# Linear attention in a fused attention and expert layer: head sums laid out place first, with the key sums as a ninth place, and the projection written to the other parity's bank

## The reference

```python
def _linear_attention(x, Wq, bq, Wk, bk, Wv, bv, Wo, bo):
    B, S, D = x.shape; H = 16; hd = D // H            # hd = 8
    v = (x @ Wv + bv).reshape(B, S, H, hd)
    q = elu((x @ Wq + bq).reshape(B, S, H, hd)) + 1.0
    k = elu((x @ Wk + bk).reshape(B, S, H, hd)) + 1.0
    def step(carry, qkv):                             # over the 256 tokens
        s, z = carry; q_i, k_i, v_i = qkv
        s = s + einsum('bhd,bhm->bhdm', k_i, v_i)
        z = z + k_i
        qs = einsum('bhd,bhdm->bhm', q_i, s)
        qz = einsum('bhd,bhd->bh', q_i, z)[..., None]
        return (s, z), qs / (qz + 1e-06)
    ...
    return values @ Wo + bo

x = x + layernorm(linear_attention(layernorm(x)))
x = x + layernorm(ffn(layernorm(x)))                  # shared expert + top-1 of 16
```

## Time and profile before

| | us |
|---|---|
| median of three runs | 351.48 |
| the profiled execution | 353.47 |
| its span, first to last instruction | 351.6 |
| stage 1, to the last quotient of attention | about 154 |
| busy over the span: PE, DVE, ACT, POOL | 266.0, 284.8, 188.8, 193.1 |

### The profile page before, as it was taken

The page is one execution under the profiler, slowest core; times in us unless marked ns, Lnnn a source line. Parts: engine busy times, 40 slices in busy tenths (PEclk is TensorE's granted clock), DMA queues, the critical chain, the costliest instruction groups (busy, mean ns, idle before and its releaser), DMA issues.

```text
span 351.6 us, 6328 instructions
## 1 busy us (share of the span) xinstructions
PE 266.0 (76%) x1493; PEld 189.3 (54%) x1493; DVE 284.8 (81%) x1147; ACT 188.8 (54%) x572; POOL 193.1 (55%) x221
## 2 busy tenths in 40 slices
PE   0449899999999995838887988730999999999100
PEld 0215565565656552524555755520999988988000
DVE  3599999999999999996998786560279999999940
ACT  1723566565656652447666563301799888885000
POOL 5064677777677773300055556371006888888870
PEclk9998999999999999877999899965699999999855
DMA  4999960000000000000011111126960101110100
GB/s 112 334 427 348 352 203 0 2 3 0 2 0 2 2 0 0 1 3 0 0 63 61 62 62 61 62 76 196 358 207 15 34 30 36 39 36 32 31 2 0
DMA packets 20275, 28.60 MB, mean 81 GB/s; under 512 B 2285, under 2 KB 15476, under 8 KB 19856
## 3 DMA queue, kind: packets, MB, share of 16 engines
q1 hardware_dynamic: 16624, 21.57, 18.2%
q0 software_dynamic: 3040, 6.37, 5.3%
q10 hardware_dynamic: 576, 0.26, 0.3%
HBM read 15.57 MB, written 13.60 MB: 83 GB/s over the span
## 4 chain that ended last, share of the span: by engine, by line
PE 39%; DVE 21%; POOL 17%; issue 12%; DMA 5%; ACT 1%; another core or an unknown queue 1%; SPq 1%; POOLq 0%; ACTq 0%; DVEq 0%
PE banks L1019 13%; POOL out L484 10%; POOL rows L478 5%; PE banks L1042 5%; DMA rows<-in_x 4%; PE banks L1106 3%; PE banks L1140 2%; PE banks L1048 2%; DVE hT L824 2%; POOL sorted_rows L468 2%; PE banks L1007 2%; PE banks L1040 1%; PE banks L1065 1%; PE banks L1063 1%; DVE stats L859 1%
## 5 line engine op out<-in xcount | busy, mean ns | idle before, releaser
L443 POOL TENSOR_TENSOR kv<-qk,vv 128x1024 f32<-128x1024 f32 x32 | 62.5, 1952 | 2.5
L1019 PE MATMUL banks<-kv,upto 128*128 128x512 f32 x128 | 61.3, 602 | 0.8 <-POOL kv L443 0.8
L1140 PE MATMUL banks<-xsT,w_now 128*128 128x128 f32 x376 | 53.8, 288 | 0.4 <-issue 0.4
L484 POOL DMA_INDIRECT out<-rows,token_i x47 | 46.9, 998 | 9.6 <-issue 8.0
L437 POOL TENSOR_TENSOR qk<-ex,rl 128x256 f32<-128x256 f32 x32 | 23.3, 729 | 50.4 <-ACT ex L542 50.4
L1140 PEld LDWEIGHTS banks<-xsT,w_now 128*128 128x128 f32 x376 | 48.1, 200 | 1.2 <-issue 0.5
L468 POOL DMA_INDIRECT sorted_rows<-rows,slot_i x32 | 31.6, 986 | 30.2 <-DVE slot_i L814 22.2
L728 DVE TENSOR_TENSOR prod<-banks,qk 128x1024 f32<-128x1024 f32 x32 | 38.9, 1217 | 2.7 <-PE banks L1019 0.8
L750 DVE TENSOR_REDUCE num<-prod 128x128 f32<-128x1024 f32 x32 | 38.7, 1208 | 0.3 <-DVE den L745 0.3
L958 DVE TENSOR_TENSOR hT_e<-silu_e,banks 128x256 f32<-128x256 f32 x47 | 19.3, 412 | 19.6 <-ACT silu_e L619 14.9
L478 POOL TENSOR_TENSOR rows<-rows,yn 128x128 f32<-128x128 f32 x40 | 19.2, 481 | 28.4 <-DVE yn L950 26.6
(11 more groups left out here) (152 smaller groups left out, 660.6 us busy)
## 6 DMA issues: line engine op xcount, KB each, us to landing
sorted_rows<-rows SPq DMA_DIRECT2D x3, 1950.0 KB, 12.0
rows<-sorted_rows SPq DMA_DIRECT2D x11, 520.0 KB, 6.2
w_exp<-in_gate_up SPq DMA_DIRECT2D x4, 1024.0 KB, 9.2
w_exp_down<-in_down SPq DMA_DIRECT2D x8, 256.0 KB, 8.8
out<-rows,token_i POOLq DMA_INDIRECT x47
rows<-in_x SPq DMA_DIRECT2D x1, 512.0 KB, 8.9
sorted_rows<-rows,slot_i POOLq DMA_INDIRECT x32
rows<-sorted_rows SPq DMA_DIRECT2D x1, 390.0 KB, 5.4
```

The costliest lines, as they stand in the source:

```text
L443: nc.gpsimd.tensor_tensor(kv[:, u, :].rearrange("p (h m d) -> p h m d", h=NH, m=HD), k, v, ALU.mult).then_inc(s_kv, 1)
L484: nc.gpsimd.indirect_dma_start(out=out_rows, out_offset=bass.IndirectOffsetOnAxis(ap=token_i[:, j - 1:j], axis=0), in_=rows[:, j - 1, 0:D] ...
L1019: ins = nc.tensor.matmul(ps_s[u % 2][:, cols], upto[:], kv[:, u, cols], start=True, stop=True)
L1140: ins = nc.tensor.matmul(ps_gue[u % 2][:, c * P:(c + 1) * P], w_now[:, u % 2, c * P:(c + 1) * P], xsT[:, u % 2, :], start=True, stop=True)
```

## The change

In words:

- The columns of a head group are laid out place first: `kv`, the sums and the outputs have the place m of v outermost and the head inside it, instead of the head outermost. The host reorders the columns of Wv and bv and the rows of Wo to match, and `head_start`, the mask's source, is laid out alike by one iota instead of two.
- k is projected ahead of q. `kv`, k and q of a tile stand in one SBUF tensor `kvq`, and the k sums are written by TensorE behind the kv sums, as columns 1,024 to 1,151 of one PSUM tensor of three banks. So q times the sums is one product of 1,152 columns, and the head sums one reduction to 144 columns: 128 numerators and 16 denominators.
- For an odd tile one addition of 144 columns brings in the carried part of both; then, for odd and even tiles alike, a tensor_scalar of 16 columns from SBUF to SBUF adds the small constant to the denominator.
- TensorE does the kv sums first, then the total state (even), then the k sums, and one semaphore says that all are there. The total state is written where v of the next tile was, so this waits for v of tile t + 1.
- The projection of tile t + 2 goes to the bank of the other parity, and waits for the product of tile t - 1 (and in an odd step for the carry of t - 1), instead of for the k product of tile t.
- VectorE's order in a step is the reciprocal of t - 1, the product of t, the carry (even), the quotient of t - 1, the sums of t, the addition (odd), the constant.

The diff, cut to its core:

```diff
-        qk = sb("qk", [P, 4, 2 * D])
-        kv = sb("kv", [P, 4, KVW])
-        zq = sb("zq", [P, D])
-        prod = sb("prod", [P, KVW])
-        num = sb("num", [P, D])
+        kvq = sb("kvq", [P, 4, KVW + 2 * D])
+        prod = sb("prod", [P, KVW + D])
+        sums = sb("sums", [P, 2, CW])
...
+        Z0, K0, Q0 = KVW, KVW, KVW + D
-        ps_qkv = [bank[0], bank[1]]
-        ps_s = [pair[1], pair[2]]
+        ps_s = [trio[0][:, 0:KVW + D], trio[1][:, 0:KVW + D]]
+        ps_qkv = [trio[0][:, KVW + D:KVW + 4 * D], trio[1][:, KVW + D:KVW + 4 * D]]
...
 # GpSimd
-                at_least(pool, s_s, t - 2)
+                at_least(pool, s_s, t - 3)
-                k = qk[:, u, D:2 * D].rearrange("p (h o d) -> p h o d", h=NH, o=1).to_broadcast([P, NH, HD, HD])
-                v = vv[:, u % 2, 0:D].rearrange("p (h m o) -> p h m o", h=NH, o=1).to_broadcast([P, NH, HD, HD])
+                k = kvq[:, u, K0:K0 + D].rearrange("p (o h d) -> p o h d", h=NH, o=1).to_broadcast([P, HD, NH, HD])
+                v = vv[:, u % 2, 0:D].rearrange("p (m h o) -> p m h o", h=NH, o=1).to_broadcast([P, HD, NH, HD])
...
 # VectorE
+                if live(t - 1, NT):
+                    dve.wait_ge(s_den, t)
+                    nc.vector.reciprocal(rden[:], den[:]).then_inc(s_recip, 1)
+                    other()
                 if live(t, NT):
-                    dve.wait_ge(s_z, t + 1)
-                    nc.vector.tensor_tensor(zq[:], ps_qkv[u % 2][:, 3 * D:4 * D], qk[:, u, 0:D],
-                                            ALU.mult).then_inc(s_chain, 1)
+                    dve.wait_ge(s_s, t + 1)
+                    nc.vector.tensor_tensor(
+                        prod[:].rearrange("p (m c) -> p m c", c=D),
+                        ps_s[u % 2].rearrange("p (m c) -> p m c", c=D),
+                        kvq[:, u, Q0:Q0 + D].rearrange("p (o c) -> p o c", o=1).to_broadcast([P, HD + 1, D]),
+                        ALU.mult).then_inc(s_prod, 1)
                     other()
                 if u % 2 == 0 and live(t, NT):
                     nc.vector.tensor_tensor(carry[:], ps_qkv[0][:, 0:CW], head_mask[:], ALU.mult)...
...
+                    dve.wait_ge(s_prod, t + 1)
+                    nc.vector.tensor_reduce(sums[:, u % 2, :], prod[:].rearrange("p (n d) -> p n d", d=HD), AX,
+                                            ALU.add).then_inc(s_sums, 1)
                     other()
+                    dve.wait_ge(s_sums, t + 1)
+                    if u % 2:
+                        dve.wait_ge(s_carried, t // 2 + 1)
+                        nc.vector.tensor_tensor(sums[:, 1, :], sums[:, 1, :], ps_xT[:, 2 * D:2 * D + CW],
+                                                ALU.add).then_inc(s_added, 1)
+                        other()
+                        dve.wait_ge(s_added, t // 2 + 1)
+                    nc.vector.tensor_scalar(den[:], sums[:, u % 2, D:CW], EPS_DEN, None, ALU.add).then_inc(s_den, 1)
...
 # TensorE
+                    pe.wait_ge(s_kv, t + 1)
+                    at_least(pe, s_prod, t - 1)
                     for half in range(2):
                         cols = slice(half * 512, (half + 1) * 512)
-                        ins = nc.tensor.matmul(ps_s[u % 2][:, cols], upto[:], kv[:, u, cols], start=True, stop=True)
-                    ins.then_inc(s_s, 1)
+                        nc.tensor.matmul(ps_s[u % 2][:, cols], upto[:], kvq[:, u, cols], start=True, stop=True)
+                    pe.wait_ge(s_v, min(t + 2, NT))
+                    if not odd:
+                        nc.tensor.matmul(ps_qkv[0][:, 0:CW], kvq[:, u, K0:K0 + D], vv[:, 0, :], start=True, stop=True)
+                    nc.tensor.matmul(ps_s[u % 2][:, Z0:Z0 + D], upto[:], kvq[:, u, K0:K0 + D],
+                                     start=True, stop=True).then_inc(s_s, 1)
                 if not odd and live(t - 1, NT):
-                    pe.wait_ge(s_chain, CH * t)
+                    pe.wait_ge(s_added, t // 2)
...
-                    at_least(pe, s_chain, CH * t + Z_READ[odd])
-                    nc.tensor.matmul(ps_qkv[u % 2][:, 0:3 * D], ones_bf[:], bias_rows[:, 0:3 * D],
+                    at_least(pe, s_prod, t)
+                    if odd and live(t, NT):
+                        pe.wait_ge(s_carry, t // 2 + 1)
+                    nc.tensor.matmul(ps_qkv[1 - u % 2][:, 0:3 * D], ones_bf[:], bias_rows[:, 0:3 * D],
                                      start=True, stop=False)
```

More of the change, by code:

```diff
@@ L272, in build @@
         token_i = sb("token_i", [P, ST], I32)
-        pair = [ctx.enter_context(nc.psum_tensor(f"banks{2 * i}", [P, 1024], F32)) for i in range(4)]
-        bank = [pair[i // 2][:, 512 * (i % 2):512 * (i % 2 + 1)] for i in range(8)]
+        trio = [ctx.enter_context(nc.psum_tensor(f"banks{3 * i}", [P, 1536], F32)) for i in range(2)]
+        last_two = ctx.enter_context(nc.psum_tensor("banks6", [P, 1024], F32))
+        bank = [trio[i // 3][:, 512 * (i % 3):512 * (i % 3 + 1)] for i in range(6)]
+        bank += [last_two[:, 0:512], last_two[:, 512:1024]]
         CHUNKS = [(0, 4), (4, 12), (12, NT)]
@@ L387, in _ @@
                 if c == 0:
-                    for n, w in enumerate((wq, wk, wv)):
+                    for n, w in enumerate((wk, wq, wv)):
                         sp.dma_start(w_qkv[:, n * D:(n + 1) * D], w).then_inc(s_w, 16)
@@ L423, in _ @@
             nc.gpsimd.iota(row_index_less[:], [[0, 1]], 1 - HD, 1, **whole)
-            nc.gpsimd.iota(head_start[:, 0:D].rearrange("p (h d) -> p h d", h=NH), [[HD, NH], [0, HD]], 0, 0, **whole)
-            nc.gpsimd.iota(head_start[:, D:CW], [[HD, NH]], 0, 0, **whole).then_inc(s_iota, 1)
+            nc.gpsimd.iota(head_start[:].rearrange("p (m h) -> p m h", h=NH), [[0, HD + 1], [HD, NH]], 0, 0,
+                           **whole).then_inc(s_iota, 1)
             nc.gpsimd.iota(row_start[:], [[0, 1]], 0, P, **whole).then_inc(s_iota, 1)
@@ L491, in _ @@
         def _(act):
-            for n, b in enumerate((bq, bk, bv, bo)):
+            for n, b in enumerate((bk, bq, bv, bo)):
                 act.dma_start(bias[:, n * D:(n + 1) * D],
@@ L709, in other @@
                         next(others, None)
-                multiplied = S_READ[u % 2]
-                if live(t, NT):
-                    dve.wait_ge(s_z, t + 1)
-                    nc.vector.tensor_tensor(zq[:], ps_qkv[u % 2][:, 3 * D:4 * D], qk[:, u, 0:D],
-                                            ALU.mult).then_inc(s_chain, 1)
-                    other()
-                if u % 2 == 0 and live(t, NT):
-                    nc.vector.tensor_tensor(carry[:], ps_qkv[0][:, 0:CW], head_mask[:], ALU.mult).then_inc(s_chain, 1)
-                    other()
                 if live(t - 1, NT):
-                    dve.wait_ge(s_chain, CH * (t - 1) + S_READ[1 - u % 2] + 3)
-                    nc.vector.reciprocal(rden[:], rden[:]).then_inc(s_recip, 1)
+                    dve.wait_ge(s_den, t)
+                    nc.vector.reciprocal(rden[:], den[:]).then_inc(s_recip, 1)
                     other()
@@ L1027, in step1 @@
                 if odd and live(t, NT):
-                    nc.tensor.transpose(ps_xT[:, D:2 * D], qk[:, u, 0:D], ident[:]).then_inc(s_q_t, 2)
+                    nc.tensor.transpose(ps_xT[:, D:2 * D], kvq[:, u, Q0:Q0 + D], ident[:]).then_inc(s_q_t, 2)
                 if live(t - 2, NT):
@@ L1115, in _ @@
             pe.wait_ge(s_xnT, NT)
[L1116 removed]
+            pe.wait_ge(s_added, NT // 2)
             step2(-1, 1)
[L1118 removed]
+            pe.wait_ge(s_prod, NT)
             pe.wait_ge(s_y_out, NT)
```

81 lines of the change are left out of this document (28 added, 53 removed).

## The result

| | before | after |
|---|---|---|
| median, us | 351.40 (4 runs) | 369.69 (4 runs, 368.19 to 369.98) |
| profiled execution | 353.47 | 369.75 |
| its span | 351.6 | 367.9 |

What follows compares the result with a forecast made beforehand. TensorE was taken to set the pace, VectorE close second. 13 loops of +1.12 gave +14.6, the start -0.5, together +14.1 on 351.48: 365.6 us, own range 360 to 370, full range 358 to 390.

Steps and rivals of the forecast that it cites:

- The hold: Even step, VectorE: the new constant, due 3.11 after the projection, waits for GpSimd's kv product and is released at 4.83.
- The loop: Even projection to next even projection through the held constant: 8.38 against 7.26, +1.12 a pair; chance 0.48.
- TensorE's work is the same; only its order and its waits change: 0: TensorE, all steps: the new order of its matmuls was claimed to cost 0.
- rival 3: Even step: the constant isn't held, pairs stay at 7.26, total 350.5 to 351.5; chance 0.10.
- The start: First steps: step 0's projection about 4 earlier; -0.5 taken, bounds a gain of 2 and a loss of 1.
- one more hold: Start of stage 1: the bound on its loss, one further held VectorE instruction, set at 1.
- The tail: Steps 26 to 29: two more loops, bounded at 0 to 3 each and taken as 1.12 each.
- GpSimd's two products keep their durations: GpSimd's two products were taken as unchanged in duration, bounds 10% either way, 0.2 a product.
- Rival 2: Odd step: the quotient is held too, loop 10.23, +2.97 a pair, 389.6 in all; chance 0.38.
- The rule beside the rows: VectorE and GpSimd: a shared-port lock held for a whole instruction; L644's pace suggested the constant might go free.
- I carry the difference over: Whole kernel: the 1.99 by which the runs' median lay below the profiled 353.47 was kept, giving a base of 351.48.

Runs made afterwards that it cites:

- e4: Kernel before plus one unused 16-column tensor_scalar on VectorE in each odd step, behind the k product: 371.74 us, ratio 1.0486 to before.
- e10: Kernel after with kv product in halves, constant added by ScalarE in even steps and within the PSUM addition in odd ones: 351.09 us, ratio 0.9938 to before.
- e12: Kernel after, kv product whole, constant added by ScalarE in even steps and within the PSUM addition in odd ones: 356.88 us, ratio 1.0118 to before.
- e5: Kernel after without the constant and with the kv product in two halves, each kv-sum matmul waiting for its own: 353.75 us, ratio 1.0014 to before.
- e1: Kernel after without the small constant on the denominator: 363.00 us, ratio 1.0228 to before.
- e9: Kernel after, constant in place, with the kv product in two halves, each kv-sum matmul waiting for its own: 356.66 us, ratio 1.0109 to before.
- e7: e5 with the projection of step 0 held back until the carry of step 0: 357.05 us, ratio 1.0084 to before.
- e2: Kernel after with the constant read through a pointer to an SBUF column instead of an immediate: 371.24 us, ratio 1.0491 to before.
- e3: Kernel after with a one-column memset ahead of each odd step's quotient: 378.98 us, ratio 1.0712 to before.
- e8: Kernel after with a 128-column memset ahead of each odd step's quotient: 379.12 us, ratio 1.0679 to before.

## Why the prediction was right, and where it was off

- **The hold.** As forecast. From the even projection at 97.24: kv product 2.86 (2.85 forecast), constant 3.14 (3.11), released 4.86 (4.83), product 5.06 (5.02), quotient 6.27 (6.23), sums 6.47 (6.43), addition 7.85 (7.80), next projection 8.58 (8.38). e4 shows the same hold alone in the kernel before, e10 and e12 its absence. TensorE's idle time for the addition was to be about 1.1 and is 0.71; another 0.26 of its waiting lies ahead of the odd step's kv sums, for the kv product (100.10 + 1.97 + 0.25 = 102.32). VectorE's own work, put at about 7.0 a pair, is borne out by e5, where it waits 0.19 of 7.22.
- **The loop was 0.12 too short.** Half of this is the last term, addition to projection: 0.31 + 0.27 forecast, 0.63 in most pairs (addition at 96.61, projection at 97.24) and 0.73 in the one shown, where from the transpose to the projection are 0.36 instead of 0.27. The other half is hundredths ahead of it, 0.05 by the addition. The mean is 8.50: 11 x 0.12 = 1.3 us.
- **"TensorE's work is the same; only its order and its waits change: 0"** was wrong, though it cost nothing in the sum. The new order, with the kv product whole, costs 0.32 a pair (7.58 against 7.26), but the loop over VectorE is longer, and hides it. e1, e5 and e12 show the cost; that it comes of the order is argued (e5). It would have been wrong by 3.5 us in rival 3, whose 350.5 to 351.5 needed more than a constant that isn't held: e12 gives 1.0118.
- **The start**, -0.5 forecast and +2.5 measured, is the largest miss of the sum. The projection of step 0 came 2.1 earlier (24.68), not 4. Then two of VectorE's instructions were held for the whole of a kv product, one of them the new constant, and TensorE rested 4.37 in step 2. VectorE, then TensorE:

```profile
27.66 1.90 DVE L94 SCALAR_TENSOR_TENSOR scratch<-stats 128x20 f32<-128x20 f32 x1
...
30.86 1.91 DVE L748 TENSOR_SCALAR den<-sums 128x16 f32<-128x16 f32 x1
```
```profile
24.68 0.33 PE L1024 MATMUL banks<-bias_rows,ones_bf 128*128 128x384 bf16 x1
...
36.58 0.47 PE L1008 MATMUL banks<-ident,xn 128*128 128x128 f32 x1 [4.37 <-DVE sums L744]
...
37.06 0.53 PE L1024 MATMUL banks<-bias_rows,ones_bf 128*128 128x384 bf16 x1
...
39.30 2.80 PE L995 MATMUL banks<-kvq,upto 128*128 128x512 f32 x4
```

  The two holds are worth 1.73 each over the 0.17 of such an instruction, 3.5 in all; before, the two holds of this stretch were a tensor_scalar of 0.71 and a tensor_tensor of 1.40, 1.8 in all. That is 1.7 more, a loss larger than the "one more hold" of 1 that was my bound. The new constant isn't what it takes: in e1, which has none, a tensor_tensor of the layernorm (L97 at 30.70) is held for 1.96 in its place, and step 4 comes at 46.80. More came behind the pause: the projection at 37.06 took 0.53 where the one at 24.68 took 0.33, and the kv sums at 39.30 took 2.80 where those of the regular stretch take 1.88. The granted clock of this stretch (24 to 44) was 0.83 on average, and 0.91 before, so TensorE worked part of it at the lower of its two levels. How much of the 2.5 is the clock's wasn't tried apart; e10 has 0.83 there too, with step 4 at 44.08. With the kv product in halves the holds are of 0.9 to 1.0 and step 4 comes at 43.7 to 44.1 (e5, e9, e10), but at 46.85 in e7; with it whole at 44.7 to 46.8 (seven kernels), and other instructions of VectorE's are held in one than in the next. e2 and e3, whose edits hardly touch the start, have it at 44.66 and 44.89, only 0.8 and 1.1 behind the kernel before. So the 2.5 is no fixed price of the change, and its cause stays open beyond the holds named here.
- **The tail**: +2.6 against 2.2. A quotient was held there (157.66, 1.94, beside the kv product of 157.48), inside the bounds of 0 to 6. The range of 360 to 370 around the forecast was narrower than its own bounds add up to: with all of them at their worst end the sum reaches 373.
- **"GpSimd's two products keep their durations"**: 1.95 became 1.97, and 2.10 to 2.12 where the quotient went free beside it; within the 10% bound, and off the loop.
- **Rival 2** was as near as it was said to be: due at 6.27 against 6.28, forecast 6.23 against 6.26. None of the 11 pairs tipped, but ten of them lie within 0.01 of the kv product's start, and e3 shows pairs tipping 0.02 behind it, at 10.3 a pair. That the forecast's case came true and not this one was luck by a hundredth or two; a chance of 0.38 was fair.
- **The rule beside the rows.** The Trainium skill (SBUF — State Buffer, Who interferes with whom) describes an exclusive lock that the first to start keeps for its whole instruction: the trace agrees, 1.72 beside 1.97, and e9's 0.96 beside a half, but for starts within 0.01 of each other, where the quotient goes free whichever is recorded first. The constant is held with an immediate (L748) and with a pointer (e2) as scalar. L644, the tensor_scalar that spoke for its going free, meets no instruction of GpSimd's, so whether one of its pace is held isn't shown.
- **"I carry the difference over"** was the second miss: of the 18.3 between the medians 2 are that the profiled execution of before lies 2.0 above its runs and that of after 0.1. The sum should have been made without it: 353.47 + 14.1 = 367.6, 2.1 below the 369.7 measured. Those 2.1 are small because misses cancel: start +3.0, pairs +1.3, tail +0.3, stages 2 and 3 -2.4.
- Stages 2 and 3 came out 2.4 shorter with no edit there. Stage 2 took 78.1 to 83.0 in the profiles of this study, so nothing is read from that.

## What to carry to other kernels

Before adding a small instruction to VectorE, look up where it falls beside GpSimd's: not its 0.17 counts but the time from its place to the end of GpSimd's instruction, and what stands behind it. Where it can't be moved, issue the GpSimd work in smaller pieces (1.72 became 0.88, but the kernel before only lost by it), or give the instruction to ScalarE or fold it into one that reads PSUM; and when an order on TensorE is changed, ask what used to run under a wait. When a loop is taken away, the next one can be only a few tenths shorter: here 8.50, 7.58 and 7.22.

## What the runs showed of the hardware that was not expected

- Who is held is decided within a hundredth or two: a quotient that starts from 0.01 ahead of the kv product to 0.01 behind it is free every time (after, e3); 0.02 behind, two were held for 2.09 (e3) and one went free (e2). The quotient costs the other little: GpSimd's 1.97 becomes 2.10 to 2.19.
- With a memset of VectorE's right ahead of it, a quotient that starts up to 0.14 behind the kv product goes free as well, and at 0.15 it is held (e8). Why isn't shown.
- From the end of a kv product to the start of the matmul that waits for it are 0.25 (e1), and 0.06 from the end of VectorE's addition to its transpose (after).
- Two products of 512 columns take 2.11 where one of 1,024 takes 1.97, and with their waits at halves this is a gain in the kernel after and a loss in the one before.
